# Silu mixtures of a 12-stage network on one core: every expert over every token, or tokens sorted by expert into 15 tiles

## The reference, cut to what matters

```python
logits = silu(xt @ rw1 + rb1) @ rw2 + rb2          # 8 experts
_, idx = top_k(logits, 2)
w = softmax(where(mask, logits, -inf), axis=1)     # only the two chosen are not 0
h = silu(einsum('nd,edh->enh', xt, we1) + be1[:, None, :])     # D=128, H=512, all experts
eo = einsum('enh,ehd->end', h, we2) + be2[:, None, :]
y = xt + einsum('ne,end->nd', w, eo)
```

## Time and profile before

| | |
|---|---|
| three runs | 2915.81, 2917.68, 2919.92 us |
| profiled execution, first to last instruction | 2916.5 us |
| what lies around it, median less span | 1.2 us |
| PE, PEld, DVE, ACT, POOL busy | 94, 41, 57, 45, 14% |
| the two L1 stages | 684.1 to 931.3 and 1709.7 to 1958.1 us |
| HBM read, written | 144.41, 19.00 MB |

### The profile page before, as it was taken

The page is one execution under the profiler, slowest core; times in us unless marked ns, Lnnn a source line. Parts: engine busy times, 40 slices in busy tenths (PEclk is TensorE's granted clock), DMA queues, the critical chain, the costliest instruction groups (busy, mean ns, idle before and its releaser), DMA issues. The chain is left out here.

```text
span 2916.5 us, 35872 instructions
## 1 busy us (share of the span) xinstructions
PE 2733.2 (94%) x12233; PEld 1208.0 (41%) x12320; DVE 1664.0 (57%) x2650; ACT 1309.1 (45%) x2678; POOL 405.0 (14%) x441
## 2 busy tenths in 40 slices
PE   7979999989998799999999989999999969999978
PEld 3446666654444222222222234444444544444433
DVE  5778898853223888888888512233332443332454
ACT  3652333334545488888887854441110131102244
POOL 1234666510002400000000000000000000000012
PEclk9988999999999699999999999999999989999999
DMA  1343322110010321110200030022211111221212
GB/s 67 102 139 114 97 97 90 58 69 30 30 51 8 91 31 22 22 31 4 40 13 3 3 122 29 30 85 74 87 66 44 37 59 58 88 73 39 64 32 73
DMA packets 78598, 165.57 MB, mean 57 GB/s; under 512 B 13504, under 2 KB 45632, under 8 KB 75552
## 3 DMA queue, kind: packets, MB, share of 16 engines
q1 hardware_dynamic: 78456, 163.76, 18.6%
HBM read 144.41 MB, written 19.00 MB: 56 GB/s over the span
## 5 line engine op out<-in xcount | busy, mean ns | idle before, releaser
L2327 DVE TENSOR_REDUCE big<-psum 128x2 f32<-128x1024 f32 x512 | 603.9, 1221 | 77.3 <-PE psum L2139 73.4
L2287 ACT ACTIVATE probs<-psum 128x512 f32<-128x512 f32 x1024 | 553.2, 600 | 138.5 <-PE psum L2160 127.0
L2160 PE MATMUL psum<-big,k_ops 128*128 128x512 bf16 x945 | 295.0, 387 | 12.0 <-ACT probs L2287 6.7
L845 PE MATMUL psum<-xn,big 128*128 128x512 f32 x512 | 237.3, 604 | 9.3 <-ACT probs L905 7.2
L1063 PE MATMUL psum<-big 128*128 128x512 f32 x512 | 232.7, 606 | 11.1 <-DVE big L1194 11.1
L854 PE MATMUL psum<-probs,big 128*128 128x512 f32 x512 | 230.8, 595 | 0.0
L944 DVE SCALAR_TENSOR_TENSOR weighted<-psum,big 128x512 f32<-128x512 f32 x64 | 48.1, 751 | 317.4 <-PE psum L854 294.5
L1088 PE MATMUL psum<-probs,big 128*128 128x512 f32 x512 | 222.0, 594 | 4.6 <-issue 3.6
L1077 PE MATMUL psum<-big 128*128 128x512 f32 x512 | 224.4, 594 | 0.0
L2160 PEld LDWEIGHTS psum<-big,k_ops 128*128 128x128 bf16 x1024 | 81.5, 97 | 335.2 <-ACT probs L2287 263.5
L905 ACT ACTIVATE probs<-psum,big 128x512 f32<-128x512 f32 x256 | 171.8, 687 | 81.3 <-PE psum L845 75.5
(11 more groups left out here) (444 smaller groups left out, 3628.9 us busy)
## 6 DMA issues: line engine op xcount, KB each, us to landing
big<-row_store SPq DMA_DIRECT2D x128, 512.0 KB, 4.1
big<-step_rows SPq DMA_DIRECT2D x16, 1024.0 KB, 4.7
qkv_chunks<-big SPq DMA_DIRECT2D x48, 256.0 KB, 2.3
big<-qkv_chunks SPq DMA_DIRECT2D x16, 768.0 KB, 4.4
big<-since_rows SPq DMA_DIRECT2D x32, 256.0 KB, 5.4
big<-row_store SPq DMA_DIRECT2D x32, 256.0 KB, 4.9
big<-in_L SPq DMA_DIRECT2D x1, 6224.0 KB, 17.6
big<-in_L SPq DMA_DIRECT2D x1, 4197.0 KB, 13.4
```

Source lines behind the costliest of these rows:

```text
L845: pe.matmul(k.bank[3 + m % 3][:, :], w["we1"][:, e, c, :], xn[:, bass.ts(n, TB)], start=True, stop=True).then_inc(pre.sem, 1)
L2160: pe.matmul(k.bank[2 + m % 3][:, :], k_ops[:, g % 2, h, kt * P:(kt + 1) * P], q_ops[:, g % 2, i % QB, h, :], start=True, stop=True).then_i ...
L2287: act.activation(probs[:, kt % 2, h, :], k.bank[2 + m % 3][:, :], ACT.Exp, scale=SCALE).then_inc(expd.sem, 1)
L2327: dve.tensor_reduce(into, k.row_pair[hp].rearrange("p (h t) -> p h t", h=2), AX.X, ALU.max).then_inc(row_max.sem, 1)
```

## The change

`top2_silu_ffn` is replaced by `sorted_silu_ffn`, and for this stage `Route` by `Dispatch`. A block's 512 tokens make 1024 (token, expert) pairs. They are sorted by expert into slots, 128 to a tile, every expert starting a new tile. That never takes more than 8 + 7 = 15 tiles, and 15 are always worked through, each with one expert.

- Where a pair goes is found by counting: PE multiplies the 0/1 picks with a triangle matrix (`pe_rank`), DVE derives the slot number and each tile's expert (`dve_place`).
- Tokens are turned to rows (`turn_tokens`), and POOL writes them to DRAM at their slots, 128 rows of 512 B to an indirect DMA, eight to a block (`scatter`). Per DRAM buffer eight DMAs fill 1024 rows; the rest keep older rows, and at the start both buffers are cleared.
- SP reads the slots back in four DMAs (`bring_slots`), PE turns them (`turn_slots`), ACT copies them out.
- An expert's weights and biases (1156 columns of f32 on 128 partitions) are read from DRAM for every tile into a ring of six, at an address that SP computes from a register (`bring_expert`).
- A tile is 4 + 4 matmuls of 128 columns and four silus of 128 columns; DVE adds the bias into `y`.
- y goes to DRAM in four DMAs (`keep_y`), POOL gathers it back by token in eight (`gather`), DVE weighs and adds the two halves (`mix`), PE turns the sum, DVE adds it to x.

The tanh of half the logit difference takes the place of the softmax's exp. The stages before L1 (`Ahead`) now also rank and place block 0. The L1 weights are no longer loaded beforehand; the L2 and A2 weights that follow the sixth stage are loaded in 14 pieces each at most. Semaphores are shared between stages that don't overlap.

```diff
+EXPERTS = 8
+SLOT_TILES = 2 * TPB + EXPERTS - 1
+EXPERT_COLS = 2 * 4 * P + 4 + D
@@ class Dispatch
+    def pe_rank(self, pe, n):
+
+        k, picked = self.k, self.d.picked
+        pe.wait_ge(self.picked.sem, self.picked.at(n))
+        pe.matmul(self.bank1[:, 0:5 * EXPERTS], k.before, picked[:, :, :].rearrange("p j e -> p (j e)"), start=True, stop=False)
+        for j in range(TPB):
+            mm = pe.matmul(self.bank1[:, (j + 1) * EXPERTS:5 * EXPERTS].rearrange("p (j e) -> p j e", e=EXPERTS), k.mean,
+                           picked[:, j, :].unsqueeze(1).to_broadcast([P, TPB - j, EXPERTS]), start=False, stop=(j == TPB - 1))
+        mm.then_inc(self.ranked.sem, 1)
...
@@ Opening, run beside the first stage
+    def clear_slots(self, sp):
+        k = self.k
+        for rows in k.slot_rows:
+            sp.dma_start(rows.rearrange("(t p) d -> p t d", p=P),
+                         k.probs[:, 0:SLOT_TILES * D].rearrange("p (t d) -> p t d", d=D)).then_inc(k.stored, 16)
+        sp.wait_ge(k.stored, 32)
@@ -top2_silu_ffn  +sorted_silu_ffn: SP
+            def bring_expert(g, e):
+                sp.dma_start(ring[g % RING], k.experts[:, bass.ds(e * EXPERT_COLS, EXPERT_COLS)]).then_inc(expert_here[g % RING].sem, 16)
+            def bring_slots(n, group):
+                g, a, b = groups[group]
+                if group == 0:
+                    sp.wait_ge(put[n % 2].sem, dma(put[n % 2], 8 * (n // 2 + 1)))
+                if n > 0:
+                    sp.wait_ge(slots_turned.sem, slots_turned.at(4 * (n - 1) + g))
+                sp.dma_start(slots[:, a:b, :], k.slot_rows[n % 2][a * P:b * P, :].rearrange("(t p) d -> p t d", p=P)
+                             ).then_inc(slots_here[g].sem, 16)
+
+            def keep_y(n, group):
+                g, a, b = groups[group]
+                sp.wait_ge(y_out.sem, y_out.at(n * TILES + b - 1))
+                sp.dma_start(k.y_rows[n % 2][a * P:b * P, :].rearrange("(t p) d -> p t d", p=P), y[:, a:b, :]).then_inc(y_kept[g].sem, 16)
...
+            for n in range(NB):
+                for m in range(TILES):
+                    g = n * TILES + m
+                    if g + RING <= LAST:
+                        sp.wait_ge(y_out.sem, y_out.at(g))
+                        if m + RING == TILES:
+                            experts = experts_of(n + 1)
+                        bring_expert(g + RING, experts[(m + RING) % TILES])
+                    if m in (4, 8, 12):
+                        keep_y(n, m // 4 - 1)
+                    if n + 1 < NB and m in (6, 7, 9, 12):
+                        bring_slots(n + 1, (6, 7, 9, 12).index(m))
+                    if left and m % 3 == 2:
+                        region, array = left.pop(0)
+                        sp.dma_start(region, array).then_inc(k.loaded, 16)
+                    if linear and n == NB - 1 and m == 13:
+                        ahead.sp_keep(sp)
+                        ahead.sp_bring(sp)
+                keep_y(n, 3)
@@ POOL
+            def scatter(n):
+                pool.wait_ge(route.placed.sem, route.placed.at(n))
+                pool.wait_ge(tok_out.sem, tok_out.at(n))
+                if n > 1:
+                    for here in slots_here:
+                        pool.wait_ge(here.sem, dma(here, n - 1))
+                for i in range(2 * TPB):
+                    pool.indirect_dma_start(k.slot_rows[n % 2][:, :], bass.IndirectOffsetOnAxis(ap=d.row[:, n, i:i + 1], axis=0),
+                                            tokens[:, n % 2, i % TPB, :], None).then_inc(put[n % 2].sem, 16)
+
+            def gather(n):
+                for kept in y_kept:
+                    pool.wait_ge(kept.sem, dma(kept, n + 1))
+                pool.wait_ge(y_mixed.sem, y_mixed.at(n - 1))
+                for i in range(2 * TPB):
+                    pool.indirect_dma_start(y_back[:, i, :], None, k.y_rows[n % 2][:, :],
+                                            bass.IndirectOffsetOnAxis(ap=d.row[:, n, i:i + 1], axis=0)).then_inc(y_here.sem, 16)
+
+            scatter(0)
+            scatter(1)
+            for n in range(NB):
+                if n + 2 < NB:
+                    scatter(n + 2)
+                gather(n)
@@ PE
+                n, m = g // TILES, g % TILES
+                here = expert_here[g % RING]
+                pe.wait_ge(here.sem, dma(here, g // RING + 1))
+                pe.wait_ge(hid.sem, hid.at((g - 1) * C - 1))
+                if m % 4 == 0:
+                    pe.wait_ge(slots_out.sem, slots_out.at(4 * n + m // 4))
+                for c in range(C):
+                    mm = pe.matmul(k.bank[3 + g % 2][:, c * P:(c + 1) * P], ring[g % RING][:, c * P:(c + 1) * P], turned[:, m, :],
+                                   start=True, stop=True)
+                mm.then_inc(pre.sem, 1)
+
+            def second_layer(g):
+                pe.wait_ge(y_out.sem, y_out.at(g - 2))
+                for c in range(C):
+                    pe.wait_ge(hid.sem, hid.at(g * C + c))
+                    mm = pe.matmul(k.bank[6 + g % 2][:, 0:D], hidden[:, g % 2, c, :],
+                                   ring[g % RING][:, C * P + c * D:C * P + (c + 1) * D], start=(c == 0), stop=(c == C - 1))
+                mm.then_inc(y_ready.sem, 1)
...
+            turn_tokens(0)
+            for step in ("centre", "variance", "spread", "hidden", "tokens", "logits", "by_token"):
+                prepare(1, step)
+            turn_slots(0, 0)
+            first_layer(0)
+            prepare(1, "rank")
+            for n in range(NB):
+                for m in range(TILES):
+                    g = n * TILES + m
+                    if g < LAST:
+                        first_layer(g + 1)
+                    if n + 2 < NB:
+                        prepare(n + 2, {0: "centre", 1: "variance", 3: "spread", 5: "hidden", 6: "logits", 7: "by_token",
+                                        8: "tokens", 10: "rank"}.get(m))
+                    if m in (1, 5, 9):
+                        turn_slots(n, (m + 3) // 4)
+                    elif m == 13 and n + 1 < NB:
+                        turn_slots(n + 1, 0)
+                    elif m == 14 and n > 0:
+                        turn_y(n - 1)
+                    if early and n > 1:
+                        next_norm(n - 2, {2: "centre", 4: "variance", 6: "spread"}.get(m))
+                    elif linear and n == NB - 1:
+                        next_norm(0, {0: "centre", 2: "variance", 4: "spread", 6: "logits", 7: "by_token", 11: "turn"}.get(m))
@@ ACT
+            def hidden_of(g):
+                act.wait_ge(pre.sem, pre.at(g))
+                act.wait_ge(y_ready.sem, y_ready.at(g - 2))
+                for c in range(C):
+                    act.activation(hidden[:, g % 2, c, :], k.bank[3 + g % 2][:, c * P:(c + 1) * P], ACT.Silu,
+                                   bias=ring[g % RING][:, 2 * C * P + c:2 * C * P + c + 1]).then_inc(hid.sem, 1)
@@ DVE
+            def out_y(g):
+                n, m = g // TILES, g % TILES
+                dve.wait_ge(y_ready.sem, y_ready.at(g))
+                if m % 4 == 0 and n > 0:
+                    kept = y_kept[m // 4]
+                    dve.wait_ge(kept.sem, dma(kept, n))
+                dve.tensor_tensor(y[:, m, :], k.bank[6 + g % 2][:, 0:D], ring[g % RING][:, 2 * C * P + C:EXPERT_COLS],
+                                  ALU.add).then_inc(y_out.sem, 1)
...
+            def mix(n):
+                dve.wait_ge(y_here.sem, dma(y_here, 8 * (n + 1)))
+                share = d.share[:, n, :, :].rearrange("p i j -> p (i j)")
+                dve.tensor_tensor(weighted[:, :, :, :].rearrange("p i j d -> p (i j) d"), y_back[:, :, :],
+                                  share.unsqueeze(2).to_broadcast([P, 2 * TPB, D]), ALU.mult)
+                dve.drain()
+                dve.wait_ge(y_turned.sem, y_turned.at(n - 1))
+                dve.tensor_tensor(mixed[:, :, :], weighted[:, 0, :, :], weighted[:, 1, :, :], ALU.add).then_inc(y_mixed.sem, 1)
+
+            def add_to_x(n):
+                xb = k.x[:, bass.ts(n, TB)]
+                dve.wait_ge(y_turned.sem, y_turned.at(n))
+                dve.scalar_tensor_tensor(xb, k.bank[5][:, :], 0.5, xb, ALU.mult, ALU.add).then_inc(x_done.sem, 1)
@@ DVE order, per block and tile
+                for m in range(TILES):
+                    g = n * TILES + m
+                    out_y(g)
+                    if n + 2 < NB:
+                        prepare(n + 2, {2: "invert", 4: "norm", 8: "first", 9: "second", 10: "weigh", 11: "place"}.get(m))
+                    if m == 1 and n > 1:
+                        add_to_x(n - 2)
+                    elif m == 6:
+                        add_input(n)
+                    elif m == 13 and n > 0:
+                        mix(n - 1)
+                    if early and n > 1:
+                        next_norm(n - 2, {5: "invert", 7: "norm"}.get(m))
+                    elif linear and n == NB - 1:
```

(6 more changed lines are left out.)

463 lines of the change are left out of this document (312 added, 151 removed).

## The result

The changed kernel takes 2876.4 us (median of 4 runs, 2872.0 to 2879.8) against 2918.8 us (2915.8 to 2920.3): ratio 0.9856, 95% interval 0.9842 to 0.9869, 42 us faster. The prediction was 2813 us, 106 us faster; the time lies in its range of 2750 to 2900, but the gain is two fifths of the one forecast.

What follows compares the result with a forecast made beforehand. PE's matmuls were taken to bound the kernel. Each changed stage was 19 + 156 + 19 = 194 us; two make 388, plus 3, less 495.6: -104.6 from 2916.5, 2811.9 profiled, 2813 us measured; range 2750 to 2900.

Steps and rivals of the forecast that it cites:

- POOL: `scatter` and `gather`: 16 indirect DMAs a block at 1.3 us, 21 us, hidden under a block's 39 us.
- Which engine is the bound, and what it costs: Middle of a stage: PE bounds with 141.7 us, 35 a block, covering ACT's 28 us a block.
- The pitch: Time between PE's 128-column matmul records in tiles: 0.12 us, bounds 0.111 and 0.133; 115.2 us for 60 tiles.
- The friction of 14 us a stage: PE held up between tiles by ACT's table loads and copies and DVE's picks and places: 3.5 us a block.
- Ends: Ahead of a stage's first tile and behind its last: 19 us each, for rows stored, scattered, gathered and turned.
- DMA: Expert, slot and y transfers: 2.44 us a tile, under PE's 2.6, so costed at nothing in the middle.
- Rival 1: POOL's indirect DMAs in `scatter` and `gather` set the pace: at 3 us each +126 us, 2939 us; chance 0.12.
- Rival 2: Tiles wait for late experts: 2900 us, half of it 2856; a lower clock alike, 2907; chance 0.22 together.
- Rival 3: Everything lean: indirect DMAs of 0.6 us, matmul records 0.111 us apart, half the friction: 2760 us; chance 0.18.
- PE over 85% busy: Sign in the profile after: PE's busy share in the middle of the two changed stages.
- about 2.6 us: Sign in the profile after: time from one tile to the next in the changed stages.
- near 75%: Sign in the profile after: ACT's busy share in the middle of the two changed stages.

Runs made afterwards that it cites:

- Spread: Changed kernel, but POOL waits for a tile's end before each indirect DMA instead of issuing runs of eight; 2819.1 us, ratio 0.9656.

## Why the prediction was wrong

The step that failed is **POOL**: "16 of them are 21 us a block, under the 39 of a block". The durations were right (1.26 us each with the gap, 1.3 forecast), the queue was never late, and so the DMAs were counted as hidden. But what ran beside them was not left alone: PE's signals were. The term that stood at nothing costs 57 us. Spread alone takes them back and lands at 2819 where 2813 was forecast, the tiles at 157.6 and 156.4 us where 156 stood. No other step of the sum is off by more than 8 us a stage in that kernel; the half clock that the sum lacked adds 12 and 7. That the time of the changed kernel lies in the stated range says nothing for the mechanism: the range was drawn for other reasons.

- *Which engine is the bound, and what it costs.* Right in sum, in part by luck, as two misses cancel. The pitch was my lower bound: 1.79 us from tile to tile of 16 records, 0.112 each:

```profile
881.13 1.06 PE L1100 MATMUL psum<-turned,big 128*128 128x128 f32 x8
...
882.92 1.06 PE L1100 MATMUL psum<-turned,big 128*128 128x128 f32 x8
```

  that is 107 us a stage, not 115. Stretches at half clock (granted 0.93 and 0.97 over the tiles of spread), which the sum didn't have, took 12 and 7 us, so PE's busy time was 145 and 140 against 141.7. The friction of 14 us a stage was 12 and 16.
- *Ends.* Right: 19.4 and 18 to 19 us. They are now 38 us a stage with hardly any tile work, which shorter runs could not touch.
- *DMA.* "At nothing" was right for PE's waits in the fourth stage of the changed kernel (0.5 us). Once the holds are gone it is wrong by up to 5 and 8 us a stage, of which 4.6 us in the sixth stage are PE's waits for late experts; for the rest, the later landings of slots and y are the likely way, not a shown one.
- *Rival 1* had the right place and the wrong mechanism: I asked how long an indirect DMA is, and never what it does to the others. *Rival 2* (2856 to 2907) had the time and was wrong in both halves: with the experts' bytes away the holds stay, and the lower clock (0.90 in the tiles) comes behind PE's standing still (4.5 us of it, then 6.5 us at 0.53), it doesn't start it. *Rival 3* was not needed; the pitch alone was lean.
- *The signs named beforehand.* "PE over 85% busy" failed (82%), "about 2.6 us" from tile to tile failed (3.06), ACT "near 75%" was 51% (94 us over the tiles, 23 a block, where I had 28; four silus take 1.14 us, where I had 1.3), "hardly waiting for big's DMA" held, and none of the reasons listed for a failure was the one.

What stays open: why the indirect form holds PE's signals and those of no other engine (none of DVE's or ACT's was late in the same stretches); why nothing was held on chip C; and the 4 to 7 us that the stages behind the sixth take more in nearly all experiments.

## What to carry to other kernels

A queue that is off the path in time can still be on it: ask of a new kind of instruction not only whether it fits beside the rest but what runs of it do to the signals of the others, and space them out by a wait on the consumer's pace. In a profile, a wait that ends on "remote", or an engine that takes up two results at once long after their recorded ends, is the sign of such a hold, whatever the busy shares say; that "remote" is missing doesn't prove that nothing is held (17 late signals with the rank later, and no "remote"). And a sum that is right in each duration can still be wrong by two fifths, so the first experiment is the one that keeps all the work and changes only its spacing.

## What was not expected of the hardware

- Runs of indirect DMAs of 128 rows (0.95 us each, 0.30 between) made TensorE's completion signals late, and no other engine's: by up to 2.9 us in runs of four, 7.1 in runs of eight and 14.8 in a run of sixteen, and what was held to the end went out about 1, 2 and 3 us behind the run. Nearly single ones, at the pace of a tile, made 7 signals late, by 1.2 us at most. On a third chip five and six in a row made none late.
- In the run of sixteen TensorE's matmuls stood too: eight that wait for nothing took 4.8 us.
- Plain DMAs of the same rows from the same engine took 0.53 us each and held nothing.
- POOL's 512-column adds stretched a VectorE step from 192 to 1034 ns.
